# A routing stage whose token list is summed in fp32r, with its weighted tiles made by two engines and its masks made earlier

## What is computed

```python
logits = x @ Wr + br                              # 8192 tokens x 8 experts
top_vals, top_idx = jax.lax.top_k(logits, 2)
w = jax.nn.softmax(top_vals, axis=-1)             # two weights for each token
key_mat = jnp.where(flat_idx[None, :] == jnp.arange(E)[:, None], w_flat[None, :], NEG)
kv, ki = jax.lax.top_k(key_mat, cap)              # each expert keeps its best cap = 1280
tok = flat_tok[ki]                                # the token list of each expert
xe = x[tok]                                       # gathered rows, then W1, gelu, W2, scatter-add
```

## Time and profile before

| | us |
|---|---|
| median of 3 runs | 1625.9 (1625.34 to 1626.49) |
| the profiled execution, its own time | 1625.48 |
| its span in the trace | 1623.7 |
| `setup` and `attention`, up to | 1180 |
| `route`, of which its list loop and closing matmul | 1180 to 1339, 1277.88 to 1337.90 |
| `experts` and `last_norm` | 1339 to the end |

### The profile page before, as it was taken

The page is one execution under the profiler, slowest core; times in us unless marked ns, Lnnn a source line. Parts: engine busy times, 40 slices in busy tenths (PEclk is TensorE's granted clock), DMA queues, the critical chain, the costliest instruction groups (busy, mean ns, idle before and its releaser), DMA issues. The chain is left out here.

```text
span 1623.7 us, 24084 instructions
## 1 busy us (share of the span) xinstructions
PE 1327.1 (82%) x5919; PEld 937.7 (58%) x5920; DVE 1145.3 (71%) x2512; ACT 740.7 (46%) x1442; POOL 556.0 (34%) x928
## 2 busy tenths in 40 slices
PE   6499999999999999999999999999511595979200
PEld 3266666666666666666666666666411595868200
DVE  2368877778777787777877778777367744656387
ACT  1366656556565565655656556564200003333052
POOL 1101423234232342323423234223310356667247
PEclk7599999999999999999999999999855556989655
DMA  4000011010110101101011010110120103232464
GB/s 108 14 14 27 1 53 49 4 52 0 53 48 4 53 0 52 47 6 52 0 53 50 3 40 1 40 40 1 44 54 0 52 0 82 36 85 33 116 220 142
DMA packets 68360, 70.29 MB, mean 43 GB/s; under 512 B 13568, under 2 KB 64176, under 8 KB 68160
## 3 DMA queue, kind: packets, MB, share of 16 engines
q1 hardware_dynamic: 44272, 44.82, 9.2%
q10 hardware_dynamic: 18960, 18.88, 3.5%
q0 software_dynamic: 5056, 5.85, 2.3%
HBM read 40.35 MB, written 28.92 MB: 43 GB/s over the span
## 5 line engine op out<-in xcount | busy, mean ns | idle before, releaser
L830 PE MATMUL PS<-PF,V 128*128 128x512 f32 x1024 | 523.9, 593 | 0.0
L561 ACT ACTIVATE PF<-PS 128x512 f32<-128x512 f32 x512 | 303.0, 595 | 345.0 <-PE PS L756 343.4
L733 DVE TENSOR_REDUCE NMAX<-PS 128x1 f32<-128x512 f32 x512 | 346.5, 687 | 160.7 <-PE PS L765 150.5
L755 PE MATMUL PS<-Q,K 128*128 128x512 f32 x512 | 405.8, 792 | 0.9 <-ACT PF L561 0.9
L531 POOL TENSOR_TENSOR XL<-XF,XH 128x512 fp32r<-128x512 f32 x64 | 84.2, 1316 | 445.7 <-ACT XH L636 445.7
L765 PE MATMUL PS<-K,Q 128*128 128x512 f32 x512 | 203.6, 398 | 6.0 <-DVE NMAX L733 5.9
L756 PE MATMUL PS<-Q,K 128*128 128x512 f32 x512 | 202.7, 396 | 0.0
L830 PEld LDWEIGHTS PS<-PF,V 128*128 128x128 f32 x1024 | 174.5, 189 | 36.2 <-issue 6.7
L579 ACT ACTIVATE Q<-PS 64x512 fp32r<-64x512 f32 x256 | 151.5, 592 | 67.8 <-PE PS L93 63.0
L755 PEld LDWEIGHTS PS<-Q,K 128*128 128x128 f32 x512 | 97.2, 190 | 123.5 <-issue 105.4
L756 PEld LDWEIGHTS PS<-Q,K 128*128 128x128 f32 x512 | 97.4, 190 | 121.7 <-issue 121.6
(11 more groups left out here) (286 smaller groups left out, 2534.6 us busy)
## 6 DMA issues: line engine op xcount, KB each, us to landing
X<-in_L_attn_x SPq DMA_DIRECT2D x16, 512.0 KB, 5.0
MODB<-mod_rows SPq DMA_DIRECT2D x16, 512.0 KB, 4.4
h_rows<-H ACTq DMA_DIRECT2D x16, 512.0 KB, 3.1
acc_rows<-H ACTq DMA_DIRECT2D x16, 512.0 KB, 4.1
A<-acc_rows SPq DMA_DIRECT2D x16, 512.0 KB, 8.3
out_x<-X SPq DMA_DIRECT2D x16, 512.0 KB, 2.9
W1F<-in_L_ffn_W SPq DMA_DIRECT2D x3, 1024.0 KB, 4.9
W2F<-in_L_ffn_W SPq DMA_DIRECT2D x3, 1024.0 KB, 5.8
```

The lines of the kernel that those rows point to most:

```text
L561: s_exp.done(act.activation(PF[:, u % 4, :], st_bank(u), ACT.Exp))
L733: s_mred.done(dve.tensor_reduce(NMAX[:, h % 2, c:c + 1], mx_bank(u), AX.X, ALU.max, negate=True))
L755: pe.matmul(st_bank(u), K1[:, kp, keys], Q1[:, h, :], start=True, stop=False)
L830: s_pv.done(pe.matmul(pv_bank(h), V1[:, vp, c, :], PF[:, u % 4, :], start=(c == 0), stop=(c == TC - 1)))
```

## The change

- In `setup`, GpSimd makes `DIFF` as its very first instruction, and VectorE makes `DIFM`, `SAME` and `LOWER` before it waits for TensorE. `SAME` and `LOWER` now live in the kernel's permanent tiles. In `route`, VectorE waits for one constant (`RANK8`) and goes straight to the logits; TensorE's wait for the masks is gone.
- `OB` and `OA` are fp32r. So that the token numbers can be held in that type, `TOK1` counts from the middle (token + 1 - 4096, from -4095 to 4096). The one token whose number would be 0 gets 6144 instead, by two new GpSimd instructions.
- `OA` is made by two engines: GpSimd takes 5 of the 8 columns in one instruction, ScalarE the other 3 in one instruction each, with the token number as its scale. TensorE waits for both.
- At the end two VectorE instructions are added, which turn 6144 back, and the constants are shifted by 4096.

```diff
@@ setup @@
+                pool.iota(DIFF[:, :], pattern=[[1, P]], base=P, channel_multiplier=-1).then_inc(s_diff, 1)
                 pool.memset(IDENT[:, :], 0.0).then_inc(s_id, 1)
...
-                chain = Chain(dve, s_dve)
+                chain, mask = Chain(dve, s_dve), Chain(dve, s_mask)
+                dve.wait_ge(s_diff, 1)
+                mask(dve.tensor_scalar(DIFM[:, :], DIFF[:, :], E - 1, None, ALU.bitwise_and))
+                mask(dve.tensor_scalar(m["SAME"][:, :], DIFM[:, :], 0.0, None, ALU.is_equal))
+                mask(dve.scalar_tensor_tensor(out=m["LOWER"][:, :], in0=DIFF[:, :], scalar=float(P), in1=m["SAME"][:, :],
+                                              op0=ALU.is_gt, op1=ALU.mult))
                 dve.wait_ge(s_pe, PE_SILU_T)
@@ route, tiles @@
-    OB, OE, OA = sb("OB", [P, 2, RING, P]), sb("OE", [P, 2, RING, SLOTC]), sb("OA", [P, 2, RING, SLOTC])
+    OB, OE, OA = sb("OB", [P, 2, RING, P], F32R), sb("OE", [P, 2, RING, SLOTC]), sb("OA", [P, 2, RING, SLOTC], F32R)
+    RPOOL = 5
+    MID, AT_MID = NT // 2, 3.0 * NT / 4
@@ route, GpSimd @@
-            link(pool.iota(DIFF[:, :], pattern=[[1, P]], base=P, channel_multiplier=-1))
...
+            tok = TOK1[:, :, :].rearrange("p j n -> p (j n)")
+            link(pool.tensor_scalar(ZTOK[:, :], tok, 0.0, AT_MID, ALU.is_equal, ALU.mult))
+            link(pool.tensor_tensor(tok, tok, ZTOK[:, :], ALU.add))
...
-                    pool.tensor_tensor(OA[:, par, :, :], OE[:, par, :, :],
-                                       tok[:, bass.ds(j * RING, RING)].unsqueeze(2).broadcast_to([P, RING, SLOTC]),
+                    pool.tensor_tensor(OA[:, par, 0:RPOOL, :], OE[:, par, 0:RPOOL, :],
+                                       tok[:, bass.ds(j * RING, RPOOL)].unsqueeze(2).broadcast_to([P, RPOOL, SLOTC]),
                                        ALU.mult).then_inc(s_oa, 1)
@@ route, ScalarE, after KT @@
+            with act.Fori(0, STEPS // 2) as i:
+                for par in range(2):
+                    j = i * 2 + par
+                    act.wait_ge(s_oe, j + 1)
+                    for r in range(RPOOL, RING):
+                        act.activation(OA[:, par, r, :], OE[:, par, r, :], ACT.Copy,
+                                       scale=tok[:, bass.ds(j * RING + r, 1)]).then_inc(s_oact, 1)
@@ route, TensorE @@
-            pe.wait_ge(s_dve, MASKS_DONE)
...
                     pe.wait_ge(s_oa, i * 2 + (par + 1))
+                    pe.wait_ge(s_oact, i * (2 * (RING - RPOOL)) + (par + 1) * (RING - RPOOL))
@@ route, VectorE @@
-            dve.wait_ge(s_pool, 7)
-            link(dve.tensor_scalar(DIFM[:, :], DIFF[:, :], E - 1, None, ALU.bitwise_and))
-            link(dve.tensor_scalar(SAME[:, :], DIFM[:, :], 0.0, None, ALU.is_equal))
-            link(dve.scalar_tensor_tensor(out=LOWER[:, :], in0=DIFF[:, :], scalar=float(P), in1=SAME[:, :],
-                                          op0=ALU.is_gt, op1=ALU.mult))
+            dve.wait_ge(s_pool, 1)
...
             link(dve.tensor_scalar(LF[:, :], list_ps, 0.0, SPARE[:, :], ALU.is_equal, ALU.mult))
-            link(dve.scalar_tensor_tensor(out=m["IDX"][:, :], in0=list_ps, scalar=-1.0, in1=LF[:, :], op0=ALU.add, op1=ALU.add))
+            link(dve.tensor_scalar(LM[:, :], list_ps, AT_MID, -AT_MID, ALU.is_equal, ALU.mult))
+            link(dve.tensor_tensor(LF[:, :], LF[:, :], LM[:, :], ALU.add))
+            link(dve.scalar_tensor_tensor(out=m["IDX"][:, :], in0=list_ps, scalar=float(MID - 1), in1=LF[:, :], op0=ALU.add,
+                                          op1=ALU.add))
```

More of the change, by code:

```diff
@@ L128, in build_program @@
         m["LOGITS"] = sb("LOGITS", [P, NCH, E])
+        m["SAME"], m["LOWER"] = sb("SAME", [P, P]), sb("LOWER", [P, P])
         with ExitStack() as attn:
@@ L171, in setup @@
         MA = sb("MA", [NB, 2, D]); ZERO = sb("ZERO", [P, D])
+        DIFF, DIFM = sb("DIFF", [P, P], I32), sb("DIFM", [P, P], I32)
         s_in, s_w, s_id, s_const, s_out = (sem(x) for x in ("s_in", "s_w", "s_id", "s_const", "s_setout"))
         s_pe, s_act, s_dve, s_mr = (sem(x) for x in ("s_setpe", "s_setact", "s_setdve", "s_mr"))
+        s_diff, s_mask = sem("s_diff"), sem("s_mask")
         MODS_DONE, AL_DONE = 13, 17
@@ L858, in route @@
     KT, JUNK, GT, EQT, SEL, SCAN, DST, ZT = (sb(x, [P, T]) for x in ("KT", "JUNK", "GT", "EQT", "SEL", "SCAN", "DST", "ZT"))
-    DIFF, DIFM = sb("DIFF", [P, P], I32), sb("DIFM", [P, P], I32)
-    SAME, LOWER, ONES = sb("SAME", [P, P]), sb("LOWER", [P, P]), sb("ONES", [P, P])
+    SAME, LOWER, ONES = m["SAME"], m["LOWER"], sb("ONES", [P, P])
     DIGU, DIGF = sb("DIGU", [P, NDIG + 1, 4], U32), sb("DIGF", [P, NDIG])
@@ L871, in route @@
     TOK1, IOT = sb("TOK1", [P, 2, NCH]), sb("IOT", [P, P])
-    OB, OE, OA = sb("OB", [P, 2, RING, P]), sb("OE", [P, 2, RING, SLOTC]), sb("OA", [P, 2, RING, SLOTC])
+    OB, OE, OA = sb("OB", [P, 2, RING, P], F32R), sb("OE", [P, 2, RING, SLOTC]), sb("OA", [P, 2, RING, SLOTC], F32R)
+    RPOOL = 5
     ZP = sb("ZP", [P, P])
-    SPARE, LF = sb("SPARE", [P, 1]), sb("LF", [P, SLOTC])
+    SPARE, LF, LM = sb("SPARE", [P, 1]), sb("LF", [P, SLOTC]), sb("LM", [P, SLOTC])
+    ZTOK = sb("ZTOK", [P, 2 * NCH])
+    MID, AT_MID = NT // 2, 3.0 * NT / 4
     NBR, NBD = sb("NBR", [1, 6, E]), sb("NBD", [P, E])
@@ L880, in route @@
     s_ob, s_oa, s_mm, s_list, s_nb, s_dd = (sem(x) for x in ("s_rob", "s_roa", "s_rmm", "s_rlist", "s_rnb", "s_rdd"))
+    s_oact = sem("s_roact")
     s_db, s_ab, s_oe, s_info = sem("s_rdb"), sem("s_rab"), sem("s_roe"), sem("s_rinfo")
-    POOL_CONSTS, MASKS_DONE = 7 + 4 * NDIG + 5, 3
+    POOL_CONSTS = 8 + 4 * NDIG + 5
     kt_ps = PS[:, 0, :]
@@ L900, in _ @@
             link(pool.iota(RANK8[:, :], pattern=[[-1, E]], base=E, channel_multiplier=0, allow_small_or_imprecise_dtypes=True))
-            link(pool.iota(DIFF[:, :], pattern=[[1, P]], base=P, channel_multiplier=-1))
             link(pool.iota(ECOLI[:, :], pattern=[[0, 1]], base=0, channel_multiplier=1))
             link(pool.iota(IOT[:, :], pattern=[[1, P]], base=0, channel_multiplier=0, allow_small_or_imprecise_dtypes=True))
-            link(pool.iota(SPARE[:, :], pattern=[[0, 1]], base=NT + 1, channel_multiplier=1, allow_small_or_imprecise_dtypes=True))
+            link(pool.iota(SPARE[:, :], pattern=[[0, 1]], base=NT + 1 - MID, channel_multiplier=1, allow_small_or_imprecise_dtypes=True))
             for j in range(2):
-                link(pool.iota(TOK1[:, j, :].rearrange("p (a b) -> p a b", a=TC), pattern=[[P, TC], [TC * P, NS]], base=1,
+                link(pool.iota(TOK1[:, j, :].rearrange("p (a b) -> p a b", a=TC), pattern=[[P, TC], [TC * P, NS]], base=1 - MID,
                                channel_multiplier=1, allow_small_or_imprecise_dtypes=True))
+            tok = TOK1[:, :, :].rearrange("p j n -> p (j n)")
+            link(pool.tensor_scalar(ZTOK[:, :], tok, 0.0, AT_MID, ALU.is_equal, ALU.mult))
+            link(pool.tensor_tensor(tok, tok, ZTOK[:, :], ALU.add))
             for d in range(NDIG):
@@ L916, in _ @@
             pool.memset(ONES[:, :], 1.0).then_inc(s_pool, 1)
-            tok = TOK1[:, :, :].rearrange("p j n -> p (j n)")
             with pool.Fori(0, STEPS // 2) as i:
```

## The result

The changed kernel takes 1605.59 us in the median of 4 runs (1602.54 to 1607.25), the kernel before 1625.62 (1622.47 to 1626.49). The ratio is 0.9878, interval 0.9858 to 0.9898: 20.0 us faster, where 21.3 were forecast (1604.6 against 1605.6). The profiled execution took 1605.83 us, its span is 1604.1.

A forecast was written before the change was run, and what follows sets the result against it. TensorE was taken to bound the list loop, and a VectorE chain everything in route before it. Gains of 17.1 (loop) and 4.8 (start) minus 0.6 behind the loop make 21.3 us: 1625.9 becomes 1604.6, range 1600 to 1611.

The forecast's parts named there:

- The list loop: List loop: VectorE and GpSimd in turn set a step of 2.51 us; 60.06 us become 42.96, a gain of 17.1.
- The check that TensorE's answer closes in time: List loop: TensorE's answer takes 2.13 us against 2.37 allowed, so OE loses nothing up to 0.24 us a matmul.
- my signs of being wrong: List loop: OE waiting for TensorE every step, OA under 0.5 us behind OB, stretched compares, ScalarE products over 0.5 us.
- The matmul: List loop: one fp32r matmul with 80 columns costs 0.21 us, taken from a 256-column row; 8 take 1.7 us.
- The start: Start of route: first read of the logits moves from 1185.95 to 1180.8, 5.15 us; gain 4.8 after 0.35 lost.
- the collision with GpSimd's two new instructions: Start of route: they read SBUF and hold up VectorE's two-input compares by 0 to 0.7 us, taken as 0.35.
- `setup`: In setup: if DIFM is held until GpSimd is quiet, masks are done by about 9.1 us; cover 1 us, cost 0.
- Behind the loop: After the list loop: two more VectorE instructions lose 0.6 us (0.5 to 0.7).
- TensorE as the bound: Rival, list loop: fp32r gives nothing at 80 columns, 0.44 us a matmul; only 4.2 us gained, 1621.7; chance 0.08.
- Memsets holding the compares: Rival, start of route: GpSimd's memsets hold VectorE's compare; 1.0 us gained instead of 4.8, time 1608.4; chance 0.10.
- VectorE alone: Rival, list loop: GpSimd's smaller piece slips between; a step of 1.88 us, 9.5 us less, 1595; chance 0.05.
- table load: Rival, list loop: each ScalarE instruction brings a 1283 ns table load; step 4.65 us, 13.9 us slower, 1640; chance 0.03.

The follow-up runs named there:

- four_buffers_5: The changed kernel with four buffers of OB, OE and OA instead of two, GpSimd still making 5 columns: loop 43.31 us against 43.35, one execution 1601.68 us.
- four_buffers_3: The changed kernel with four buffers instead of two and GpSimd making 3 columns instead of 5: loop 39.02 us, one execution 1598.09 us.
- memsets_held: The kernel before, with GpSimd's memsets in route waiting until VectorE has made its masks: one execution 1624.49 us, against the profiled 1625.48 of before.

## Why the prediction was right

The mechanism was right in both places. That the touched pieces come so near the sum, 21.33 against 21.3 us, is partly luck: the loop gained 0.4 us less than forecast (15 steps of 2.53 instead of 2.51, and the 0.24 below), and the start 0.37 more.

**The list loop** went from 60.06 to 43.35 us, forecast 42.96. The terms: GpSimd behind `OB` 0.72 (taken at 0.70, bounds 0.57 and 0.75), `OE` behind GpSimd 0.68, `OB` 1.13, a matmul 0.21. The step that carried it was to read the pace after the change from the only two steps of before in which TensorE had not yet been the bound. That GpSimd and VectorE take turns is shown by four kernels: the step follows GpSimd's share (2.93, 2.53, and with four buffers 2.26 and 2.13 us for 8, 5, 3 and 2 columns) and doesn't move when TensorE's work is halved.

**The check that TensorE's answer closes in time** had two terms too small, and it didn't matter here. I took 0.15 us from GpSimd's end to the first matmul, and it is 0.24. And I took 8 x 0.21 + 0.30 = 1.98 us from there to `OE`, where it is 2.07: the 0.30 came from 16 records at 0.22, and with 0.213 it is 0.40. The first `OE` behind TensorE comes at 1281.18, and to lose nothing it had to be issued by 1281.39 - 0.14 = 1281.25. So the spare was 0.07 us, not 0.24. With 3 columns, where it counts, the 0.24 was the miss; the 2.07 I had by then from the trace. My signs were too coarse for so small a spare: `OE` waits for TensorE in 14 of 16 steps, which stands among my signs of being wrong, and it is stretched only to 0.90, not in full. Neither told the pace; half the matmuls and four buffers did. In the kernel with all 8 columns and one wait on TensorE, GpSimd's end to the first matmul of the loop is 0.15 again (1278.15 to 1278.30), and with ScalarE as the last producer 0.05. That the second wait behind the first costs the 0.1 is likely; no run changed their order.

**The matmul** was priced from a row with 256 columns, 0.21 us, and 80 columns cost the same. The f32 record with 8 columns, read as 3.56/16 = 0.22, is 0.21 too once its last record's tail is left out. So neither form pays for columns at this size; what sets the 0.21, the load of the weights or something else, no run here tells. By the Trainium skill (TensorE: Matmul & The Clock Gate, "LDWEIGHTS") a load of 128 columns takes about 107 ns; f32 records (0.213) and fp32r matmuls (0.21) at this clock both come at about twice that. The measurement decides.

**The start** won 5.16, forecast 5.15 before the 0.35 for the collision with GpSimd's two new instructions, which cost at most 0.06: the piece takes 91.92 to 91.98 in the ten kernels that have them and 91.92 or 91.93 in the three that don't. Of the bounds 0 to 0.7 the lower was right. `ZTOK`, with one SBUF input, ran from 1185.58 to 1186.26 beside a two-input compare that took 0.72 instead of 0.69; the two-input `TOK1` addition began 0.09 us before that compare's end and met only reduces. The rule of the Trainium skill (SBUF — State Buffer, "SBUF: two separate sides"), a lock between a two-input VectorE instruction and a GpSimd one that reads SBUF, would have held the compare until 1186.26; the trace shows no such hold for a GpSimd instruction with one input, and shows it for those with two.

**`setup`**: I allowed `DIFM` to be held until GpSimd was quiet, and the masks to be done by about 9.1 us; they were done by 2. `DIFM` took its 0.23 us although a memset (1.08 to 1.28) ran beside its start, so one memset alone did not hold it here.

**Behind the loop** 0.55 us were lost, forecast 0.6. Whether the token numbers would come through fp32r without being counted from the middle, which would save this, no run tried.

**The rivals.** TensorE as the bound is out: its 8 matmuls take 1.9 us of 2.53. Memsets holding the compares is out: 0.69 us beside them, though they did hold `DIFM`. VectorE alone is out, at 2.53 and not 1.88 us. ScalarE brought no table load: three products take 0.86 us.

**Where 21.3 became 19.6 in the profiled executions.** In untouched code. The larger part stands at the end of `attention`, where TensorE does four groups of 12 matmuls, each group behind VectorE. The granted clock there, before and after:
```profile
1155.00:1160.00 5.00, 3.85 (x26) 3.36 (x26) 2.54 (x8) 0.00 (x0) 0.00 (x0) 0.89 0.00 0
1160.00:1165.00 5.00, 2.35 (x19) 1.95 (x17) 2.92 (x13) 0.00 (x0) 0.14 (x1) 1.00 0.00 0
```
```profile
1155.00:1160.00 5.00, 3.86 (x18) 3.27 (x16) 1.73 (x6) 0.00 (x0) 0.00 (x0) 0.50 0.00 0
1160.00:1165.00 5.00, 4.43 (x19) 4.13 (x20) 2.08 (x7) 0.00 (x0) 0.00 (x0) 0.50 0.00 0
```
Apart from the masks in `setup` both kernels issue the same instructions up to here, at times 0.3 us apart, and TensorE had stood 4.64 us idle before in both. In the one execution its clock was back at the upper level after one group, in the other it stayed at 1.2 GHz through all four, and matmuls followed each other by 0.21 instead of 0.115 us: 3.8 us over three groups. The change is not the reason: `four_buffers_5` and `four_buffers_3`, with the same code up to here as the change, had the upper level in these groups (logits ready at 1178.60 and 1177.99), and of the kernels with the old `setup` one, `memsets_held`, had the lower. Over the profiled executions of all kernels here, the logits were ready between 1177.99 and 1184.19 us, and the piece behind `IDX` took 281.89 to 285.37, with no order in it that follows what was changed. That is the width of the runs, and it bounds what a median of a few can show: the 1.3 us between 20.0 and 21.3 can't be told from it. The difference of medians, 20.0 us, has an interval from 16.6 to 23.1 (0.0102 and 0.0142 of 1625.6), and 21.3 lies in it. Which way a single execution goes stays open; no run here steers it.

**The range.** By its own terms the lower end is 1604.6 - 2.0 - 1.7 - 0.35 - 1 = 1599.5, not 1600.5; nothing rests on it.

## What to carry to other kernels

When the bound engine gets faster, the pace that comes next may stand in the trace already, in the first steps of a pipeline, before the old bound has filled it. A wait shown ahead of an instruction says little if that instruction would be held anyway: halve the work of the engine waited for, or add buffers, and see whether the step moves. Where a kernel's gain is of the size of its own scatter, cut the span at events around the change; the pieces agreed to 0.1 us here while whole executions differed by 5.

## What was not expected of the hardware

- A row of some 60 GpSimd memsets, most of them of 0.1 us, held a one-input integer instruction of VectorE for 2.75 us, all of them together; two-input f32 compares and a one-input f32 reduce beside the same memsets were not held at all.
- TensorE counted as busy for 20.00 of 20.00 us while it was starved by some 0.2 us in every second step: in the loop the split alone, which can only bring `OA` earlier, won 1.8 us.
- An fp32r matmul with 128 weight columns took 0.21 us at 1.2 GHz for 80 columns as for 256, where an f32 one takes two records of 0.213.
- GpSimd's product against a repeated token number took 1.68 ns an element ((1.12 - 0.18) us for the 560 between 8 columns and 1), against 2.28 for two full tiles, fixed part included.
